# Layer-3 local attention: dividing after the context instead of before, with the row sums taken by TensorE

## The chip, the cores and the metric

One core of one Trainium2 chip runs the whole kernel in one launch. The metric is device time in microseconds (us), from start to end of that launch; the median of three runs stands for a kernel. One more execution was recorded by the profiler, and every duration below is from it.

## What is computed

The network has four layers, each an attention-like part times the silu of a feed-forward-like part, added to the input. The change lies in the second part of layer 3 (`_L3_ffn_ref`), which is itself a two-layer local transformer (DEPTH 2, 8 heads of 64, windows of 64 positions). Per layer of it:

```
q = l2norm(q) * qs;  k = l2norm(k) * ksc;  q, k = rotary_xpos(q, k)
sim  = einsum('bhwid,bhwjd->bhwij', 8 * bq, bk)      # keys: window before and own window, 128
sim  = where(mask, -max, sim)
attn = softmax(sim, axis=-1)
out  = einsum('bhwij,bhwjd->bhwid', attn, bv)
x = x + out @ wo ... then a layer norm and a gelu feed-forward part
```

## The kernel before, in words

The network runs in a loop of 8 chunks of 512 tokens (2 sequences of 256) for layers 0 and 1, then layer 2, then again 8 chunks for layer 3. In each of those last 8 chunks `layer3_attention` runs first and `layer3_ffn` (line 1589 on) second. `layer3_ffn` goes twice through `for l in range(DEPTH)`, so what is told here happens 16 times in a run. All data is f32, with features or queries on the 128 partitions.

Each engine has its own written-out list of instructions, in program order; nothing is scheduled by a tool. Engines wait for each other by semaphores (`wait_ge`), and `link` makes an engine wait for its own last instruction. So what stands behind a waiting instruction on its engine waits too.

One pass through `l` has four pieces. First the projections: TensorE (L1612, L1618), squares on ScalarE (L1722), rotary products on VectorE (L1789), their sums on GpSimd (L1859, L1860), the norms (L1603, L1708 to L1713) and the normalised keys and queries on VectorE (L1777). Second the **attention stage**, on which the change works. Third the output projection (L1680) and the residual sum (L1817 to L1820). Fourth layer norm and feed-forward part.

The attention stage handles A = 8 units; a unit is two heads (hp) of one sequence (sq) with 4 windows of 64 queries, laid out as 128 rows (2 heads x 64 queries) by 512 columns (4 windows x 128 keys). A unit m passes through these steps:

- **scores** (PE, L1631 and, for the mask, L1635), made for two units at once, into PSUM banks 0, 1, 5, 7. The scores of a pair need the exponentials two pairs back to be done (`win_exped`), because they take their banks.
- **row maximum** (DVE, L1803) and its product with -8 (DVE, L1805).
- **exponentials** (ACT, L1743, four instructions) into buffer PP of four slots.
- **row sum** (DVE, L1812), **reciprocal** of 4 sums per row (DVE, L1813), and **product** of the exponentials with it (POOL, L1864).
- **transposes** (PE, L1660, four of 128x128), copied from PSUM to PT by ACT (L1736).
- **context** (PE, L1674, eight products, values times PT) into bank 4 or 6. Both sequences of a head pair share a bank: 512 columns.
- **copy** of the finished head pair to OF (DVE, L1800), once per two units.

Each engine takes these steps of different units in a fixed interleaving, `for m in range(A + 4)` on PE and ACT and `range(A + 5)` on DVE: in turn m, PE makes the scores of m and m+1 (m even), the transposes of m-3 and the context of m-4; ACT copies the transposes of m-4 and then exponentiates m; DVE copies the context of m-5 (where it ends a head pair), takes the maximum of m and then the sum and reciprocal of m-1. At m = 0 and 1 DVE also makes the last two normalised tiles (L1777). After the eight products L1864 of the first layer GpSimd issues eight gathers for the next chunk (`gather_mixed`, L1430).

Of the kernel before, what the change touches and what calls it, by code (L numbers as in the profile page):

```python
# [8 lines left out]
ALU = mybir.AluOpType  # L9
ACT = mybir.ActivationFunctionType  # L10
AX = mybir.AxisListType

D = 128
SEQ = 256
NB = 2
T = NB * SEQ
# [13 lines left out]
DEPTH, LH, LD, WIN = 2, 8, 64, 64  # L30
LI = LH * LD
# [1406 lines left out]
def layer3_attention(nc, c, w, r, it, x_mid, s_mid, PB):  # L1438
    with ExitStack() as ctx:
# [20 lines left out]
        with nc.Block() as block:  # L1460
# [107 lines left out]
L3F_SEMS = (LN_SEMS + GATE_SEMS + LINKS + "pad_set shift_done raw_ready squared multiplied norm_ready norm_taken rnorm_ready "  # L1568
            "first_turned second_turned both_ready v_ready v_copied win_ready win_max win_exped win_recip prob_ready probT_ready "
            "probT_copied ctx_ready ctx_copied o_ready x_added hn_ready gate_in_ready gelu_done val_ready hid_ready "  # L1570
            "out_ready layer_done x_done xT_ready x_copied x_stored places_copied ")
NW = SEQ // WIN
SCORES = 4
SCORE_BANKS = (0, 1, 5, 7)
NT = LI // 128
# [3 lines left out]
def layer3_ffn(nc, c, ws, r, soft, it, out, ys_mid, PB):  # L1579
    with ExitStack() as ctx:  # L1580
        s = record(**semaphores(nc, ctx, L3F_SEMS)._asdict(), gathered=soft.soft0)
        b = buffers(nc, ctx, "l3f", HS=[NB, SEQ], HN=[T], SQ=[2, 2, T], CS=[2, 4, T], NR=[2, T], RN=[2, T],
                    QK=[2 * NT, T], VL=[NB, 3, LI], MX=[NW], MN=[SCORES, NW], SM=[NW], RS=[SCORES, NW], PP=[SCORES, T], PT=[2, T], OF=[NT, T],
                    G=[3, T], HH=[3, T])
        F = c.XN
        U, A, P = 2 * NT, NT * NB, NT
        VALUES = ((0, 1), (2, 3), (4,), (5,))

        with nc.Block() as block:
            @block.tensor  # L1590
            def _(pe):
                for l in range(DEPTH):
                    w, u0, a0 = ws[l], l * U, l * A
# [43 lines left out]

                    for m in range(A + 4):
                        if m < A and m % 2 == 0:
                            if m == 0:  # L1640
                                pe.wait_ge(s.multiplied, u0 + U - 2)
                            if m == 2:
                                pe.wait_ge(s.norm_taken, l * P + P)
                                pe.wait_ge(s.v_copied, NB * 3 * (l + 1))
                            if m % 4 == 0:
                                pe.wait_ge(s.both_ready, l * P + 2 * (m // 4) + 2)
                            if m >= SCORES:
                                pe.wait_ge(s.win_exped, a0 + m - SCORES + 2)
                            scores(m)
                            if m == 0:  # L1650
                                norm(P - 1)
                        v = m - 3
                        if 0 <= v < A:
                            if v == 0:
                                pe.wait_ge(s.multiplied, u0 + U)
                            pe.wait_ge(s.prob_ready, a0 + v + 1)
                            if v >= 2:
                                pe.wait_ge(s.probT_copied, a0 + v - 1)
                            for win in range(NW):
                                last = nc.tensor.transpose(PB[:, 2 + v % 2, win * 128:(win + 1) * 128],  # L1660
                                                           b.PP[:, v % SCORES, win * 128:(win + 1) * 128], c.ident)
                            last.then_inc(s.probT_ready, 1)
                        v = m - 4
                        if 0 <= v < A:
                            hp, sq = 2 * (v // 4) + v % 2, v // 2 % 2
                            if sq == 0 and hp >= 2:
                                pe.wait_ge(s.ctx_copied, l * NT + hp - 1)
                            pe.wait_ge(s.probT_copied, a0 + v + 1)
                            k = 4 + 2 * (hp % 2)
                            for win in range(NW):  # L1670
                                for h in range(2):
                                    f0 = (2 * hp + h) * LD
                                    o0 = sq * SEQ + win * WIN
                                    last = nc.tensor.matmul(PB[LD * h:LD * h + LD, k, o0:o0 + WIN], b.VL[:, sq, max(win - 1, 0), f0:f0 + LD],  # L1674
                                                            b.PT[:, v % 2, win * 128 + h * WIN:win * 128 + h * WIN + WIN],
                                                            start=True, stop=True, tile_position=(0, LD * h))
                            last.then_inc(s.ctx_ready, 1)
                    for t in range(NT):
                        pe.wait_ge(s.ctx_copied, l * NT + max(t + 1, NT - 1))
                        last = nc.tensor.matmul(PB[:, 4, :], w.o[:, t * 128:(t + 1) * 128], b.OF[:, t, :], start=t == 0, stop=t == NT - 1)  # L1680
# [20 lines left out]
            def _(act):  # L1701
                link = Link(act, s.act_link)
                act.preload_act_table_set(EXP_LN)
                for l in range(DEPTH):
# [24 lines left out]

                    for m in range(A + 4):  # L1730
                        v = m - 4
                        if v >= 0:
# [24 lines left out]
            def _(dve):  # L1757
# [10 lines left out]
                for l in range(DEPTH):  # L1768
# [25 lines left out]

                    for m in range(A + 5):
                        v = m - 5
                        if 0 <= v and v // 2 % 2:
                            hp = 2 * (v // 4) + v % 2
                            dve.wait_ge(s.ctx_ready, a0 + v + 1)
                            nc.vector.tensor_copy(b.OF[:, hp, :], PB[:, 4 + 2 * (hp % 2), :]).then_inc(s.ctx_copied, 1)  # L1800
                        if m < A:
# [5 lines left out]
                            if m < 2:  # L1807
                                normalised(P - 2 + m)
                        v = m - 1
                        if 0 <= v < A:  # L1810
                            dve.wait_ge(s.win_exped, a0 + v + 1)
                            link(nc.vector.tensor_reduce(b.SM[:], b.PP[:, v % SCORES, :].rearrange("p (w k) -> p w k", k=128), AX.X, ALU.add))  # L1812
                            nc.vector.reciprocal(b.RS[:, v % SCORES, :], b.SM[:]).then_inc(s.win_recip, 1)  # L1813
                            dve.wait_ge(s.win_recip, a0 + v + 1)
                    dve.wait_ge(s.o_ready, l + 1)
# [34 lines left out]
            def _(pool):  # L1850
# [3 lines left out]
                for l in range(DEPTH):  # L1854
                    u0 = l * U
                    for i in range(P):
                        if i < P:
                            pool.wait_ge(s.multiplied, u0 + 2 * i + 2)
                            nc.gpsimd.tensor_tensor(b.CS[:, i % 2, 0, :], b.CS[:, i % 2, 0, :], b.CS[:, i % 2, 3, :], ALU.subtract).then_inc(s.first_turned, 1)  # L1859
                            nc.gpsimd.tensor_tensor(b.CS[:, i % 2, 2, :], b.CS[:, i % 2, 2, :], b.CS[:, i % 2, 1, :], ALU.add).then_inc(s.second_turned, 1)  # L1860
                    for m in range(A):
                        pool.wait_ge(s.win_recip, l * A + m + 1)
                        pp = b.PP[:, m % SCORES, :].rearrange("p (w k) -> p w k", k=128)
                        nc.gpsimd.tensor_tensor(pp, pp, b.RS[:, m % SCORES, :].unsqueeze(2).broadcast_to([128, NW, 128]),  # L1864
                                                ALU.mult).then_inc(s.prob_ready, 1)
                    if l == 0:
# [296 lines left out]
```

## Time and profile before

| | |
|---|---|
| median of 3 runs | 4228.34 us (4226.57 to 4237.04) |
| the profiled execution: its time / its span | 4234.82 us / 4233.2 us |
| PE busy | 3121.1 us, 74% |
| DVE busy | 2419.7 us, 57% |
| ACT busy | 1756.8 us, 42% |
| POOL busy | 1192.0 us, 28% |

The span is the time from the first to the last recorded instruction, and the busy shares are means over stages with different limits. A busy share below 100% on all engines means that at each moment one of them waits for another; which one, in the stage in question, is read from the order of time.

### The profile page before, as it was taken

What the parts mean: (1) busy time and instruction counts of PE and PEld (TensorE: products, weight loads), DVE (VectorE), ACT (ScalarE), POOL (GpSimd) and SP (SyncE); (2) the same over time, 40 slices, a digit from 0 to 9 for tenths busy, and PEclk for the clock granted to TensorE, in tenths of its full rate; (3) what the DMA queues carried; (4) which work ended last, traced back from release to release, by engine and by line L of the source; (5) the groups of instructions that cost most, each with busy time, mean ns of one, the idle gap of its engine ahead of it and who ended that gap; (6) DMA issues with size and microseconds to landing.
All of it is one profiled execution on the core that took longest, in us unless ns stands there. A gap on an engine that the chain in (4) does not pass through costs nothing. (4 is left out here: it accounts for less than half of the span.)

```text
span 4233.2 us, 54691 instructions
## 1 busy us (share of the span) xinstructions
PE 3121.1 (74%) x20450; PEld 1694.0 (40%) x20450; DVE 2419.7 (57%) x3405; ACT 1756.8 (42%) x3556; POOL 1192.0 (28%) x878
## 2 busy tenths in 40 slices
PE   6788888887343778888767678676786867768687
PEld 3444444444131333444334344343443434434344
DVE  2344444444263778778855665556665565656655
ACT  2333333333132555556434434344343444535344
POOL 0000000000232454445543243332433324233242
PEclk7888888888655889999878879688796887969779
DMA  2000000000121222333300000000000000000001
GB/s 95 8 7 5 3 7 7 7 7 5 65 92 50 69 74 75 92 88 88 84 18 6 9 1 6 8 6 9 1 6 8 6 9 1 6 8 6 8 1 8
DMA packets 82171, 112.05 MB, mean 26 GB/s; under 512 B 9920, under 2 KB 47296, under 8 KB 81344
## 3 DMA queue, kind: packets, MB, share of 16 engines
q1 hardware_dynamic: 76608, 98.31, 7.7%
q0 software_dynamic: 5376, 11.02, 1.1%
q8 instruction: 145, 2.38, 0.2%
q14 instruction: 42, 0.34, 0.0%
HBM read 82.55 MB, written 26.74 MB: 26 GB/s over the span
## 5 line engine op out<-in xcount | busy, mean ns | idle before, releaser
L370 ACT ACTIVATE l_PT<-PB 128x512 f32<-128x512 f32 x512 | 277.9, 595 | 542.0 <-PE PB L281 542.0
L281 PE MATMUL PB<-l_QM,l_KP 32*128 32x256 f32 x2048 | 375.0, 496 | 131.6 <-DVE l_QM L419 76.0
L1412 POOL TENSOR_TENSOR l_ST<-l_ST,l_CT 128x1024 f32<-128x1024 f32 x128 | 316.4, 2472 | 354.3 <-DVE l_ST L1351 354.3
L408 DVE TENSOR_REDUCE keep_MXP<-PB 128x4 f32<-128x1024 f32 x256 | 301.3, 1219 | 109.1 <-PE PB L254 109.1
L1351 DVE TENSOR_TENSOR_SCAN l_ST<-l_DA,l_DB 128x1024 f32<-128x1024 f32 x128 | 355.6, 2778 | 4.4
L281 PEld LDWEIGHTS PB<-l_QM,l_KP 32*128 32x128 f32 x2048 | 242.7, 244 | 258.7 <-ACT l_PT L370 98.6
L704 POOL MEMSET l_KV<- 128x4 f32 x8 | 0.8, 104 | 941.3 <-POOLq L109 941.3
L1563 POOL TENSOR_TENSOR l_PT<-l_PT,l_PEN 128x512 f32<-128x512 f32 x168 | 213.1, 1290 | 186.0 <-ACT l_PT L370 186.0
L1345 DVE TENSOR_TENSOR l_DB<-PB,l_BT 128x1024 f32<-128x1024 f32 x128 | 155.3, 1213 | 137.5 <-PE PB L1111 137.5
L1274 ACT ACTIVATE l_DA<-PB,keep_aneg 128x510 f32<-128x510 f32 x256 | 161.1, 683 | 160.2 <-DVE l_ST L1351 83.4
L295 PE MATMUL PB<-l_PT,keep_VT 128*32 128x256 f32 x2048 | 187.6, 529 | 35.5 <-POOL l_PT L1563 25.6
L1743 ACT ACTIVATE l3f_PP<-PB,l3f_MN 128x128 f32<-128x128 f32 x512 | 145.6, 367 | 160.0 <-DVE l3f_MN L1805 160.0
L254 PE MATMUL PB<-l_KP,l_QP 32*128 32x256 f32 x2048 | 199.8, 518 | 15.6 <-issue 15.6
L1789 DVE SCALAR_TENSOR_TENSOR l3f_CS<-PB,w3fs,consts 128x512 f32<-128x512 f32 x256 | 175.2, 745 | 54.7 <-ACT l3f_SQ L1722 51.4
L1111 PE MATMUL PB<-l_DL,consts 32*128 32x512 f32 x512 | 166.0, 686 | 52.8 <-ACT l_DA L1274 37.7
L419 DVE TENSOR_TENSOR l_QM<-l_QP,PB 128x256 f32<-128x256 f32 x128 | 53.9, 421 | 258.5 <-PE PB L263 255.0
L1864 POOL TENSOR_TENSOR l3f_PP<-l3f_PP,l3f_RS 128x512 f32<-128x512 f32 x128 | 133.1, 1040 | 219.9 <-DVE l3f_RS L1813 219.9
L1859 POOL TENSOR_TENSOR l3f_CS<-l3f_CS 128x512 f32<-128x512 f32 x64 | 81.0, 1266 | 340.2 <-DVE l3f_CS L1789 340.2
L1612 PE MATMUL PB<-l3f_HS,w3fs 128*128 128x512 f32 x256 | 136.3, 659 | 35.9 <-DVE l3f_HS L1762 23.0
L1631 PE MATMUL PB<-l3f_QK 32*64 32x128 f32 x4096 | 138.8, 287 | 32.0 <-ACT l3f_NR L1708 26.0
L1111 PE MATMUL PB<-l_DU,consts 32*128 32x512 f32 x512 | 159.3, 682 | 0.0
L1449 POOL TENSOR_SCALAR l_T<-l_AJ,l_GI 128x256 f32<-128x256 f32 x16 | 18.3, 1146 | 478.8 <-DVE l_AJ L1539 478.8
(419 smaller groups left out, 6771.5 us busy)
## 6 DMA issues: line engine op xcount, KB each, us to landing
l_WB<-in_w2f_dram SPq DMA_DIRECT2D x80, 320.0 KB, 3.0
l_WB<-in_w2f_dram SPq DMA_DIRECT2D x80, 258.0 KB, 2.7
l_XR<-xs_mid SPq DMA_DIRECT2D x80, 64.0 KB, 1.8
ys_mid<-l_YO SPq DMA_DIRECT2D x80, 64.0 KB, 2.8
s_mid<-keep_S SPq DMA_DIRECT2D x17, 256.0 KB, 2.0
w3fs<-in_w3f_dram SPq DMA_DIRECT2D x1, 3127.0 KB, 18.1
keep_XI<-in_x_dram SPq DMA_DIRECT2D x9, 256.0 KB, 3.1
x_mid<-keep_X SPq DMA_DIRECT2D x9, 256.0 KB, 3.1
```

Source lines behind the costliest of these rows:

```text
L254: last = nc.tensor.matmul(PB[:, r, qt * SEQ:(qt + 1) * SEQ], b.QP[rows, a, q0:q0 + 128], b.KP[rows, a, i, sq * SEQ:(sq + 1) * SEQ], start= ...
L281: last = nc.tensor.matmul(PB[:, 4 + u % STBANKS, kt * SEQ:(kt + 1) * SEQ], b.KP[rows, a, i, k0:k0 + 128], b.QM[rows, n % 2, :], start=True ...
L295: last = nc.tensor.matmul(PB[32 * r:32 * r + 32, 7, 0:SEQ], VT[:, 2 * sq + kt, 8 * a + 2 * r + i, :], b.PT[:, (NR * (2 * j + i) + r) % PSL ...
L370: nc.scalar.activation(b.PT[:, u % PSLOTS].rearrange("p k q -> p (k q)"), PB[:, 4 + u % STBANKS, :], ACT.Exp).then_inc(s.exp_done, 1)
L408: nc.vector.tensor_reduce(dst[:, 2 * pair:2 * pair + 2, :, 16 + n % 2], PB[:, 2 * pair:2 * pair + 2, :].rearrange("p r (t k) -> p r t k", ...
L1111: return nc.tensor.matmul(PB[:, bank + e, :], c.rowsel[q:q + 32, i * 128:(i + 1) * 128], src[q:q + 32, k % 2, h, :], start=True, stop=True)
L1274: last = nc.scalar.activation(b.DA[:, g % 2, e, :].rearrange("p (s t) -> p s t", t=SEQ)[:, :, 1:SEQ], PB[:, e, :].rearrange("p (s t) -> p ...
L1345: nc.vector.tensor_tensor(b.DB[:, g % 2], PB[:, PAIR0:PAIR0 + 2, :], b.BT[:, k % 2, :].unsqueeze(1).broadcast_to([128, 2, T]), ALU.mult).t ...
L1351: nc.vector.tensor_tensor_scan(b.ST[:, g % RING].rearrange("p k t -> p (k t)"), b.DA[:, g % 2].rearrange("p k t -> p (k t)"), b.DB[:, g % ...
L1412: nc.gpsimd.tensor_tensor(b.ST[:, g % RING], b.ST[:, g % RING], b.CT[:, k % 2, :].unsqueeze(1).broadcast_to([128, 2, T]), ALU.mult).then_i ...
L1563: nc.gpsimd.tensor_tensor(pt, pt, b.PEN[:, 2 * sq:2 * sq + 2, :], ALU.mult).then_inc(s.weighed_pool, 1)
L1789: last = nc.vector.scalar_tensor_tensor(out=seq(b.CS[:, i % 2, 2 * half + j, :]), in0=seq(PB[:, 2 * (i % 2) + half, :]), scalar=scale, in1 ...
```

## The change

The exponentials are no longer divided before they are transposed. PE transposes them as ScalarE wrote them and multiplies them with the values; two more products per unit, with a matrix of ones as the stationary side (L1677 of the changed kernel), give the row sums, each sum standing on the 64 partitions of its head and on the column of its query, beside the context. DVE then takes the reciprocal of these 128x256 sums and multiplies the 128x256 context by it. GpSimd has nothing left to do in the stage. Each unit now has a bank half of its own (columns 0 to 255 for the context, 256 to 511 for the sums), and banks 4 and 6 alternate from unit to unit. The transposes, context and division of a unit each stand one turn earlier in the loops than the transposes, context and copy did.

```
@@ PE
-                    for m in range(A + 4):
+                    for m in range(A + 3):
...
-                        v = m - 3
+                        v = m - 2
...
-                            pe.wait_ge(s.prob_ready, a0 + v + 1)
+                            pe.wait_ge(s.win_exped, a0 + v + 1)
...
-                        v = m - 4
+                        v = m - 3
...
-                            if sq == 0 and hp >= 2:
-                                pe.wait_ge(s.ctx_copied, l * NT + hp - 1)
+                            if v >= 2:
+                                pe.wait_ge(s.ctx_divided, a0 + v - 1)
                             pe.wait_ge(s.probT_copied, a0 + v + 1)
-                            k = 4 + 2 * (hp % 2)
+                            k = 4 + 2 * (v % 2)
...
+                            for h in range(2):
+                                last = nc.tensor.matmul(PB[LD * h:LD * h + LD, k, SEQ:2 * SEQ], c.ones[:, 0:LD],
+                                                        b.PT[:, v % 2, :].rearrange("p (w h q) -> p h w q", h=2, q=WIN)[:, h],
+                                                        start=True, stop=True, tile_position=(0, LD * h))
                             last.then_inc(s.ctx_ready, 1)
                     for t in range(NT):
-                        pe.wait_ge(s.ctx_copied, l * NT + max(t + 1, NT - 1))
+                        pe.wait_ge(s.ctx_divided, a0 + A - (t < NT - 1))
@@ ACT
-                    for m in range(A + 4):
-                        v = m - 4
+                    for m in range(A + 3):
+                        v = m - 3
@@ DVE
-                    for m in range(A + 5):
-                        v = m - 5
-                        if 0 <= v and v // 2 % 2:
-                            hp = 2 * (v // 4) + v % 2
+                    for m in range(A + 4):
+                        v = m - 4
+                        if 0 <= v:
+                            hp, sq = 2 * (v // 4) + v % 2, v // 2 % 2
                             dve.wait_ge(s.ctx_ready, a0 + v + 1)
-                            nc.vector.tensor_copy(b.OF[:, hp, :], PB[:, 4 + 2 * (hp % 2), :]).then_inc(s.ctx_copied, 1)
+                            link(nc.vector.reciprocal(b.RD[:], PB[:, 4 + 2 * (v % 2), SEQ:2 * SEQ]))
+                            nc.vector.tensor_tensor(b.OF[:, hp, sq * SEQ:(sq + 1) * SEQ], PB[:, 4 + 2 * (v % 2), 0:SEQ], b.RD[:],
+                                                    ALU.mult).then_inc(s.ctx_divided, 1)
+                            dve.wait_ge(s.ctx_divided, a0 + v + 1)
...
-                            dve.wait_ge(s.win_exped, a0 + v + 1)
-                            link(nc.vector.tensor_reduce(b.SM[:], b.PP[:, v % SCORES, :].rearrange("p (w k) -> p w k", k=128), AX.X, ALU.add))
-                            nc.vector.reciprocal(b.RS[:, v % SCORES, :], b.SM[:]).then_inc(s.win_recip, 1)
-                            dve.wait_ge(s.win_recip, a0 + v + 1)
@@ POOL
-                    for m in range(A):
-                        pool.wait_ge(s.win_recip, l * A + m + 1)
-                        pp = b.PP[:, m % SCORES, :].rearrange("p (w k) -> p w k", k=128)
-                        nc.gpsimd.tensor_tensor(pp, pp, b.RS[:, m % SCORES, :].unsqueeze(2).broadcast_to([128, NW, 128]),
-                                                ALU.mult).then_inc(s.prob_ready, 1)
```

How this moves instructions on TensorE (PE), from the second pair of scores of a stage on; before:

```order
L1631 MATMUL PB<-l3f_QK 64x128 x32
L1635 MATMUL PB<-windowb,identb 128x512 x2
L1660 MATMUL PB<-consts,l3f_PP 128x128 x4
L1631 MATMUL PB<-l3f_QK 64x128 x32
L1635 MATMUL PB<-windowb,identb 128x512 x2
L1660 MATMUL PB<-consts,l3f_PP 128x128 x4
L1674 MATMUL PB<-l3f_PT,l3f_VL 64x64 x8
L1660 MATMUL PB<-consts,l3f_PP 128x128 x4
L1674 MATMUL PB<-l3f_PT,l3f_VL 64x64 x8
```

and now, from the same pair of scores on:

```order
L1631 MATMUL PB<-l3f_QK 64x128 x32
L1635 MATMUL PB<-windowb,identb 128x512 x2
L1660 MATMUL PB<-consts,l3f_PP 128x128 x8
L1673 MATMUL PB<-l3f_PT,l3f_VL 64x64 x8
L1677 MATMUL PB<-l3f_PT,consts 64x256 x2
L1631 MATMUL PB<-l3f_QK 64x128 x32
L1635 MATMUL PB<-windowb,identb 128x512 x2
L1660 MATMUL PB<-consts,l3f_PP 128x128 x4
L1673 MATMUL PB<-l3f_PT,l3f_VL 64x64 x8
L1677 MATMUL PB<-l3f_PT,consts 64x256 x2
```

Ahead of the third pair of scores there stood the transposes of one unit; now there stand the transposes of two units and the whole context of the first, with its two products by ones.

On VectorE (DVE), from the maximum of the fourth unit on; before:

```order
L1803 TENSOR_REDUCE l3f_MX<-PB 128x4
L1805 TENSOR_SCALAR l3f_MN<-l3f_MX 128x4
L1812 TENSOR_REDUCE l3f_SM<-l3f_PP 128x4
L1813 RECIPROCAL l3f_RS<-l3f_SM 128x4
L1803 TENSOR_REDUCE l3f_MX<-PB 128x4
L1805 TENSOR_SCALAR l3f_MN<-l3f_MX 128x4
```

and now:

```order
L1809 TENSOR_REDUCE l3f_MX<-PB 128x4
L1811 TENSOR_SCALAR l3f_MN<-l3f_MX 128x4
L1803 RECIPROCAL l3f_RD<-PB 128x256
L1804 TENSOR_TENSOR l3f_OF<-PB,l3f_RD 128x256
L1809 TENSOR_REDUCE l3f_MX<-PB 128x4
L1811 TENSOR_SCALAR l3f_MN<-l3f_MX 128x4
```

The sum and the small reciprocal of the unit before are gone from between two maxima, and the large reciprocal and the product of the unit four back have come there; the copies L1800 are gone too.

## Rows read from the trace of the kernel before

**Rows 1.** The page's head: span, busy time of each engine.
```profile
span 4233.2 us, 54691 instructions
...
PE 3121.1 (74%) x20450; PEld 1694.0 (40%) x20450; DVE 2419.7 (57%) x3405; ACT 1756.8 (42%) x3556; POOL 1192.0 (28%) x878
```
**Rows 2.** Chain of work, last attention stage: start us, us, what.
```profile
4189.59 0.69 PE PB L1674 x16
4190.27 1.91 PE PB L1631 x64
```
**Rows 3.** Timeline, last attention stage: start us, us, engine line op [idle before].
```profile
4173.03 1.98 PE L1631 MATMUL PB<-l3f_QK 32*64 32x128 f32 x64 [0.37 <-DVE l3f_QK L1777]
...
4181.68 0.68 DVE L1812 TENSOR_REDUCE l3f_SM<-l3f_PP 128x4 f32<-128x512 f32 x1
...
4187.90 0.69 DVE L1812 TENSOR_REDUCE l3f_SM<-l3f_PP 128x4 f32<-128x512 f32 x1
4187.90 1.14 ACT L1743 ACTIVATE l3f_PP<-PB,l3f_MN 128x128 f32<-128x128 f32 x4 [0.45 <-DVE l3f_MN L1805]
...
4189.98 0.69 DVE L1812 TENSOR_REDUCE l3f_SM<-l3f_PP 128x4 f32<-128x512 f32 x1
...
4205.47 0.68 DVE L1817 TENSOR_TENSOR l3f_HS<-keep_XN,PB 64x512 f32<-64x512 f32 x1 [3.10 <-PE PB L1680]
```
**Rows 4.** The same timeline: TensorE's steps and who follows them.
```profile
4192.11 0.61 PE L1635 MATMUL PB<-windowb,identb 128*128 128x512 bf16 x2
...
4192.55 0.60 PE L1660 MATMUL PB<-consts,l3f_PP 128*128 128x128 f32 x4
...
4193.08 0.69 PE L1674 MATMUL PB<-l3f_PT,l3f_VL 128*64 128x64 f32 x16
...
4193.70 0.66 PE L1660 MATMUL PB<-consts,l3f_PP 128*128 128x128 f32 x4
...
4200.19 1.44 PE L1674 MATMUL PB<-l3f_PT,l3f_VL 128*64 128x64 f32 x32
...
4200.99 1.38 DVE L1800 COPY l3f_OF<-PB 128x512 f32<-128x512 f32 x2 [2.56 <-PE PB L1674]
...
4201.73 3.70 PE L1680 MATMUL PB<-l3f_OF,w3fs 128*128 128x512 f32 x8
```
**Rows 5.** Groups by line and form: busy us, mean ns, idle before.
```profile
L1864 POOL TENSOR_TENSOR l3f_PP<-l3f_PP,l3f_RS 128x512 f32<-128x512 f32 x128 | 133.1, 1040 | 219.9 <-DVE l3f_RS L1813 219.9
...
L1803 DVE TENSOR_REDUCE l3f_MX<-PB 128x4 f32<-128x512 f32 x128 | 88.0, 687 | 44.6 <-PE PB L1635 42.4
...
L1736 ACT ACTIVATE l3f_PT<-PB 128x512 f32<-128x512 f32 x128 | 76.0, 611 | 26.8 <-PE PB L1660 26.8
...
L1800 DVE COPY l3f_OF<-PB 128x512 f32<-128x512 f32 x64 | 44.2, 692 | 64.5 <-PE PB L1674 49.8 <-remote 13.6
...
L1813 DVE RECIPROCAL l3f_RS<-l3f_SM 128x4 f32<-128x4 f32 x128 | 22.8, 178 | 4.4
...
L157 DVE SCALAR_TENSOR_TENSOR l3f_HN<-PB,keep_lnt 128x256 f32<-128x256 f32 x32 | 13.6, 424 | 1.1
...
L871 DVE TENSOR_REDUCE l2r_M<-l2r_LO 128x4 f32<-128x64 f32 x8 | 1.8, 220 | 0.3
...
L1961 DVE TENSOR_TENSOR w3fs<-w3fs,PB 128x1 f32<-128x1 f32 x4 | 0.6, 146 | 0.0
```
**Rows 6.** Line L1805: duration ns least/median/longest over all stages.
```profile
L1805 DVE TENSOR_SCALAR l3f_MN<-l3f_MX x128: 170/364/739, 2266.0 to 4195.8; 128x4 f32<-128x4 f32 x128
```
**Rows 7.** Timeline of a first-layer stage: slow scores, gathers beside a copy.
```profile
3065.92 3.44 PE L1631 MATMUL PB<-l3f_QK 32*64 32x128 f32 x64
...
3086.54 0.94 POOL L1430 DMA_INDIRECT keep_YG<-ys_mid,places  x1 [0.30 <-issue]
...
3086.91 0.69 DVE L1800 COPY l3f_OF<-PB 128x512 f32<-128x512 f32 x1 [1.43 <-remote]
```
**Rows 8.** Windows view of those scores: us, busy by engine, granted clock (PEclk), DMA.
```profile
3065.90:3069.30 3.40, 3.40 (x66) 3.05 (x65) 2.18 (x6) 2.14 (x8) 2.00 (x2) 0.55 0.02 5
```

More of the change, by code:

```diff
@@ L1568 @@
 L3F_SEMS = (LN_SEMS + GATE_SEMS + LINKS + "pad_set shift_done raw_ready squared multiplied norm_ready norm_taken rnorm_ready "
-            "first_turned second_turned both_ready v_ready v_copied win_ready win_max win_exped win_recip prob_ready probT_ready "
-            "probT_copied ctx_ready ctx_copied o_ready x_added hn_ready gate_in_ready gelu_done val_ready hid_ready "
+            "first_turned second_turned both_ready v_ready v_copied win_ready win_max win_exped probT_ready "
+            "probT_copied ctx_ready ctx_divided o_ready x_added hn_ready gate_in_ready gelu_done val_ready hid_ready "
             "out_ready layer_done x_done xT_ready x_copied x_stored places_copied ")
@@ L1582, in layer3_ffn @@
         b = buffers(nc, ctx, "l3f", HS=[NB, SEQ], HN=[T], SQ=[2, 2, T], CS=[2, 4, T], NR=[2, T], RN=[2, T],
-                    QK=[2 * NT, T], VL=[NB, 3, LI], MX=[NW], MN=[SCORES, NW], SM=[NW], RS=[SCORES, NW], PP=[SCORES, T], PT=[2, T], OF=[NT, T],
+                    QK=[2 * NT, T], VL=[NB, 3, LI], MX=[NW], MN=[SCORES, NW], RD=[SEQ], PP=[SCORES, T], PT=[2, T], OF=[NT, T],
                     G=[3, T], HH=[3, T])
@@ L1672, in _ @@
                                     f0 = (2 * hp + h) * LD
-                                    o0 = sq * SEQ + win * WIN
-                                    last = nc.tensor.matmul(PB[LD * h:LD * h + LD, k, o0:o0 + WIN], b.VL[:, sq, max(win - 1, 0), f0:f0 + LD],
+                                    nc.tensor.matmul(PB[LD * h:LD * h + LD, k, win * WIN:win * WIN + WIN], b.VL[:, sq, max(win - 1, 0), f0:f0 + LD],
                                                             b.PT[:, v % 2, win * 128 + h * WIN:win * 128 + h * WIN + WIN],
                                                             start=True, stop=True, tile_position=(0, LD * h))
+                            for h in range(2):
+                                last = nc.tensor.matmul(PB[LD * h:LD * h + LD, k, SEQ:2 * SEQ], c.ones[:, 0:LD],
+                                                        b.PT[:, v % 2, :].rearrange("p (w h q) -> p h w q", h=2, q=WIN)[:, h],
+                                                        start=True, stop=True, tile_position=(0, LD * h))
                             last.then_inc(s.ctx_ready, 1)
                     for t in range(NT):
-                        pe.wait_ge(s.ctx_copied, l * NT + max(t + 1, NT - 1))
+                        pe.wait_ge(s.ctx_divided, a0 + A - (t < NT - 1))
                         last = nc.tensor.matmul(PB[:, 4, :], w.o[:, t * 128:(t + 1) * 128], b.OF[:, t, :], start=t == 0, stop=t == NT - 1)
@@ L1808, in _ @@
                                 normalised(P - 2 + m)
-                        v = m - 1
-                        if 0 <= v < A:
-                            dve.wait_ge(s.win_exped, a0 + v + 1)
-                            link(nc.vector.tensor_reduce(b.SM[:], b.PP[:, v % SCORES, :].rearrange("p (w k) -> p w k", k=128), AX.X, ALU.add))
-                            nc.vector.reciprocal(b.RS[:, v % SCORES, :], b.SM[:]).then_inc(s.win_recip, 1)
-                            dve.wait_ge(s.win_recip, a0 + v + 1)
                     dve.wait_ge(s.o_ready, l + 1)
```

## The prediction

> **What bounds the kernel now.** I read the page's head first [rows 1]: no engine is near full, PE with 74% of 4233.2 us is the busiest, and that mean says nothing about the stage that changes. So I took the last attention stage alone: its chain of waits [rows 2] and its order of time [rows 3, 4]. From the first scores at 4173.03 to the residual sum at 4205.47 it takes 32.44 us, and there are 16 of them, some 520 us, 12% of the run. In its middle VectorE sets the pace: two row sums stand at 4187.90 and 4189.98, 2.08 us apart, and between them lie a sum, a small reciprocal, a maximum and the product with -8. The chain leaves DVE only where the order of PE and ACT forces a detour: transposes copied by ACT, context on PE, and then the next scores, which stand behind that context in PE's list [rows 2]. So there are two limits close together: DVE's own work per unit, and a loop PE, DVE, ACT, PE, ACT, PE that a unit runs through. GpSimd's product takes 1.04 us per unit and GpSimd idles 219.9 us before it [rows 5]: it is no bound, only a step on the way.
>
> **What the change takes away.** Per unit: the row sum 0.69 [rows 3], the small reciprocal 0.178, half of a 0.692 copy [rows 5], and on GpSimd 1.04 us. With the gaps that is 2.08 + 0.35 = 2.43 us of DVE per unit down to maximum and product alone. The product with -8 is at best 170 ns, but at the median 364 and at most 739 [rows 6]; it lasts longer where GpSimd works, so I give it 0.17 from here on. Maximum and product then take 0.92 us with their semaphores.
>
> **What it adds on DVE.** A product of 128x256, for which the nearest row is 0.424 us [rows 5], 0.46 with its gap, and a reciprocal of 128x256, of which the trace has no example: only one of 4 elements, 178 ns [rows 5]. This is the price that decides. Reductions give the fixed part of an instruction and its cost per element: 220 ns for 64 elements, 687 for 512 [rows 5], so 1.04 ns per element and 153 fixed. By that fixed part the reciprocal has 25 ns for four elements, 6.2 each, and 256 cost 0.153 + 1.6 = 1.75 us. If it ran at the pace of all others, one element per 1.04 ns, it would be 0.42, the lower end. If the fixed part is that of the shortest instruction with operands, 146 ns for one element [rows 5], so 145, then 33 ns are left for four, 8.2 each, and 256 cost 2.25 us, the upper end. In between lies the product with -8 of the same four elements, 170 ns [rows 6]: by it only 8 ns are extra, 3 ns per element in all, 0.95 us. I take 1.75, because reductions read one tensor and wait for nothing else, like a reciprocal, and because 0.42 leaves 20 of the 178 ns unexplained.
>
> The Trainium skill has a rule here that speaks against the change: its page "VectorE: DVE Perf Modes", section "First, the fixed hardware budget", says that Reciprocal is an iterative divide with a repeat count of 8. Read as eight cycles of the page's 0.96 GHz per element, that would be an estimated 2.28 us, the rival of the upper end below; no row here shows more than four elements.
>
> **What it adds on PE.** Two products of 256 columns per unit, each issued as two passes. A pass of 512 columns takes 0.43 us (eight of them in 3.70 [rows 4], the last one's tail included), so four passes of 256 take 0.85 one after another. But the context's 16 passes of 64 columns, 0.85 by the same rate, take 0.62 from 4193.08 to 4193.70 [rows 4]: the two halves of the array work side by side. So 0.43 to 0.85; I take 0.5.
>
> **The sum: one stage walked through.** Times are from the stage's first scores. PE's steps: scores of a pair 1.91 [rows 2] and 0.44 for the mask, 2.35; transposes 0.53; context 0.62 [rows 4] and 0.5, 1.11 together; from a context's start to DVE 0.80 [rows 4] and 0.5, so 1.3.
> - DVE finishes its last normalised tile at 8.65 (4181.68 [rows 3]); nothing before that changes. Third maximum and product: 9.6. ACT's exponentials 1.14 [rows 3] to 10.75. Behind them stands the copy of the first transposes, 0.61 [rows 5], to 11.4. Context on PE, and DVE's first reciprocal starts at 12.7.
> - Reciprocal and product take 1.75 + 0.06 + 0.46 = 2.27: 14.97, and the next maximum 15.9. Meanwhile PE does the third pair of scores, which now stand behind the context: 12.5 + 2.35, transposes 0.53, then the second context at 15.4; DVE can go on at 16.7, ends at 18.96.
> - Three turns of 0.92 + 2.27 = 3.19: 28.5. Here DVE is the bound.
> - The sixth context waits for the last exponentials and ACT's copy: DVE goes on at 29.4. Two times 2.27: 33.9. The output projection may start, its last part hides the eighth division (2.27 against 2.56). From there 3.74 us to the residual sum [rows 4]: 37.7.
>
> Against 32.44 that is +5.3; the same walk with the old order comes out at 32.7, so I take 5.1 per stage, 16 x 5.1 = +82 us.
>
> Two edits with no sum of their own. The gathers of the next chunk stood behind the eight GpSimd products in the first of the two layers; with those gone they start when the rotary sums end, about 5 us into the stage, and run for 8 x 1.25 = 10 us. Before, one copy waited 1.43 us beside them [rows 7]; now the copies are gone, and instead three products with -8 lie beside the gathers. I let one and the other cancel; if only the gain remained, it would be 8 x 1.4 = 11 us. And in that layer one pair of scores took 3.44 us, where the same step in other stages takes 1.98 [rows 7, 3]: the granted clock was 0.55 there [rows 8], close to the lower of its two levels (1.2 of 2.4 GHz), after PE had idled. Idle time now falls in two shorter pieces, because transposes come in between; at most another 8 x 1.5 = 12 us less, in which I don't trust. GpSimd's product is nowhere missed: it was off the path except for its delay, which the walk already leaves out.
>
> So 4234.82 + 82 = 4317 for the profiled execution; the median of the runs lies 6.5 below that execution: **4310 us**.
>
> **The rivals.**
> - *Eight cycles per element.* Reciprocal 2.25: each turn 3.69. The same walk gives 12.7, 15.5, 16.7, 19.5, 30.5, 30.9, 36.4, and now the eighth division ends at 39.2, later than the projection's first three parts; the residual sum at 40.4. Less the same 0.2 that is +7.8 per stage, +125: 4353. For it: the upper end of the rows. Against it: the fixed part would have to be the least seen.
> - *The reciprocal runs like any other instruction.* With 0.42 DVE is free, yet the stage isn't shorter. The third pair of scores still can't start before 12.5, because a context with its ones and the transposes of two units stand before it; the fourth starts at about 18.6, where it started at 17.2 before (4190.2 [rows 2]); the rest takes as long as before. +1.3 per stage, +21: 4249. At 0.95 it is +2.6, +42: 4270. For it: the 8 ns against the product with -8.
> - *DVE's freed time comes through* (the faster side). If DVE's work per unit is all that matters, then at 0.42 a unit costs 0.92 + 0.94 = 1.86 instead of 2.43, so 0.57 x 8 x 16 = 73 us less: 4155. It decides from a reciprocal below 0.99 us on, and needs PE's scores not to be held by the context before them. The chain through PE between 4189.59 and 4192 [rows 2] speaks against it: that detour already exists and gets longer.
> - *The change does nothing here* because all this lies beside other work: excluded, the chain of waits runs through the stage from end to end.
>
> **How the numbers follow.** Reciprocal near 1.75: 0.50. Near 2.25: 0.25. Between 0.42 and 0.95 with PE as the bound: 0.18. DVE's time comes through: 0.07. The likeliest gives 4310, with 4285 to 4335 for the ones at 0.43 to 0.85 us and the gathers either way. The range leaves out the faster side and the very lowest of the third case, and ends above 4353 by the same spread: 4250 to 4365. A measurement of this kernel can tell some 0.3% (13 us) from no change. Faster by more: 0.07. Within 0.3%: 0.05, the lowest part of the third case with the gathers' gain. Slower: 0.88.
>
> **What would show it.** In the profile after: the group of the reciprocal at 1.7 to 1.8 us mean (2.25 or 0.42 for the rivals); DVE's maxima 3.2 us apart in the middle of a stage; DVE busy up, by 128 x (1.75 + 0.42 - 0.69 - 0.18 - 0.35 - 0.16) = 101 us, to 2520; a stage of 37.5 us; PE busy up, POOL down by 133. ScalarE waiting for PE or DVE in every turn. Wrong would be the walk if the reciprocal is 1.75 and the stages are still below 35 us or above 40, and the choice of price if the reciprocal is elsewhere.

## The result and the profile after

The changed kernel takes **4317.93 us**, median of 4 runs (4311.35 to 4324.31), the kernel before 4227.45 beside it (4 runs, 4203.07 to 4237.04): ratio 1.0223, 95% interval 1.0177 to 1.0269. So it is slower, by about 94 us; 4310 was forecast. Below, a ratio leaves out executions that ran over 1.5% above the fastest of their kernel at a lower clock (one of e7's, one of e8's, two of e11's), while a median is that of all. The profiled execution took 4311.35 us. The head of its page, against [rows 1]:

```profile
span 4309.1 us, 55483 instructions
...
PE 3145.9 (73%) x20858; PEld 1707.7 (40%) x20962; DVE 2536.5 (59%) x3341; ACT 1756.8 (41%) x3556; POOL 1068.7 (25%) x750
```

DVE has 116.8 us more, POOL 123.3 less. The groups by line and form (as in [rows 5]: busy us and mean ns of one, then the engine's idle us just before them and what ended it):

```profile
L1803 DVE RECIPROCAL l3f_RD<-PB 128x256 f32<-128x256 f32 x128 | 224.9, 1757 | 90.8 <-PE PB L1677 53.5 <-remote 34.6
...
L1809 DVE TENSOR_REDUCE l3f_MX<-PB 128x4 f32<-128x512 f32 x128 | 88.0, 688 | 26.8 <-remote 22.6 <-PE PB L1635 1.7
...
L1677 PE MATMUL PB<-l3f_PT,consts 128*64 128x256 f32 x512 | 83.1, 398 | 0.0
...
L1804 DVE TENSOR_TENSOR l3f_OF<-PB,l3f_RD 128x256 f32<-128x256 f32 x128 | 54.3, 424 | 4.4
```

The price that had to be chosen is in the first row: 1757 ns per reciprocal. The column of idle time has something new beside it: 34.6 us before the reciprocals and 22.6 before the maxima end in "remote", an event that no instruction in the trace explains ("issue" stands where the engine waited for nothing that the trace shows), where the maxima of before waited for PE [rows 5].

The timeline of the last stage, the one that the prediction walked through (answers to [rows 3, 4]):

```profile
4244.07 1.98 PE L1631 MATMUL PB<-l3f_QK 32*64 32x128 f32 x64 [0.37 <-DVE l3f_QK L1780]
...
4255.34 0.69 PE L1673 MATMUL PB<-l3f_PT,l3f_VL 128*64 128x64 f32 x16 [2.02 <-ACT l3f_PT L1739]
...
4256.39 1.98 PE L1631 MATMUL PB<-l3f_QK 32*64 32x128 f32 x64
...
4256.57 1.76 DVE L1803 RECIPROCAL l3f_RD<-PB 128x256 f32<-128x256 f32 x1 [2.02 <-PE PB L1677]
...
4260.50 1.76 DVE L1803 RECIPROCAL l3f_RD<-PB 128x256 f32<-128x256 f32 x1 [0.78 <-PE PB L1677]
...
4262.75 0.69 DVE L1809 TENSOR_REDUCE l3f_MX<-PB 128x4 f32<-128x512 f32 x1
...
4265.93 0.69 DVE L1809 TENSOR_REDUCE l3f_MX<-PB 128x4 f32<-128x512 f32 x1
...
4269.11 0.69 DVE L1809 TENSOR_REDUCE l3f_MX<-PB 128x4 f32<-128x512 f32 x1
...
4277.56 3.70 PE L1683 MATMUL PB<-l3f_OF,w3fs 128*128 128x512 f32 x8 [1.13 <-DVE l3f_OF L1804]
...
4281.37 0.68 DVE L1817 TENSOR_TENSOR l3f_HS<-keep_XN,PB 64x512 f32<-64x512 f32 x1 [1.61 <-PE PB L1683]
```

The stage runs from 4244.07 to 4281.37, 37.30 us against 32.44. The first reciprocal starts 12.50 us in, the second 16.43 us in, and the maxima then stand 3.18 us apart. Between two of them the chain of waits now lies on DVE alone:

```profile
4262.30 0.43 DVE l3f_OF L1804
4262.75 0.70 DVE l3f_MX L1809
4263.48 0.18 DVE l3f_MN L1811
4263.68 1.77 DVE l3f_RD L1803
```

The windows view of whole stages, the last first-layer one and the last second-layer one; before, then after. Its columns: the stretch, its length, the busy us of PE, of PE's weight loads, of DVE, ACT and POOL (instructions in brackets), the granted clock of PE as a share of 2.4 GHz, the busy share of the DMA engines, GB/s:

```profile
4102.36:4137.57 35.21, 26.60 (x436) 18.81 (x436) 23.47 (x43) 16.93 (x46) 17.39 (x17) 0.95 0.13 9
4173.03:4205.47 32.44, 25.05 (x436) 17.51 (x436) 23.63 (x42) 16.94 (x46) 11.78 (x11) 1.00 0.01 2
```

```profile
4164.28:4208.60 44.32, 32.26 (x464) 21.44 (x468) 31.08 (x38) 16.91 (x46) 11.95 (x11) 0.88 0.23 13
4244.07:4281.37 37.30, 27.53 (x464) 18.60 (x468) 30.79 (x38) 16.76 (x46) 3.48 (x3) 1.00 0.01 2
```

Both layers have the same busy time on DVE (31.08 and 30.79 us), yet the first layer's stage is 7.0 us longer. It is the one with the gathers, and its mean clock is 0.88. Its timeline:

```profile
4169.68 1.86 POOL L1430 DMA_INDIRECT keep_YG<-ys_mid,places  x1 [0.15 <-issue]
...
4174.67 0.69 DVE L1809 TENSOR_REDUCE l3f_MX<-PB 128x4 f32<-128x512 f32 x1 [1.57 <-remote]
...
4177.28 1.12 PE L1673 MATMUL PB<-l3f_PT,l3f_VL 128*64 128x64 f32 x16 [3.76 <-issue]
...
4179.19 2.40 PE L1631 MATMUL PB<-l3f_QK 32*64 32x128 f32 x17
...
4181.84 2.86 PE L1631 MATMUL PB<-l3f_QK 32*64 32x128 f32 x47 [0.25 <-issue]
4182.04 1.76 DVE L1803 RECIPROCAL l3f_RD<-PB 128x256 f32<-128x256 f32 x1 [5.50 <-remote]
...
4187.73 1.76 DVE L1803 RECIPROCAL l3f_RD<-PB 128x256 f32<-128x256 f32 x1 [1.50 <-PE PB L1677]
...
4208.60 0.68 DVE L1817 TENSOR_TENSOR l3f_HS<-keep_XN,PB 64x512 f32<-64x512 f32 x1 [1.61 <-PE PB L1683]
```

and the same stretch in windows of 4 us:

```profile
4174.00:4178.00 4.00, 0.72 (x14) 0.72 (x16) 1.76 (x4) 2.40 (x9) 2.88 (x4) 0.79 0.78 43
4178.00:4182.00 4.00, 3.62 (x33) 1.77 (x33) 0.00 (x0) 0.86 (x3) 1.89 (x2) 0.50 0.88 40
4182.00:4186.00 4.00, 3.67 (x51) 3.20 (x53) 2.84 (x3) 0.00 (x0) 0.00 (x0) 0.50 0.63 30
```

While the gathers keep the DMA engines 0.78 to 0.88 busy, PE does 0.72 us of work in four, then runs at the lower clock level (0.50 of 2.4 GHz) for eight us.

The second reciprocal waits for PE. It starts 23.45 us into this stage and 16.43 us into the other, so all 7.0 us arise before it. On PE they are these: the first context starts 1.7 us later; from there to the third pair of scores it takes 0.9 us longer; the scores themselves take 5.5 us instead of 1.98; and 0.9 us more go by from there to the reciprocal. The scores are slow by more than their clock: in the rows above 17 of their 64 products take 2.40 us, the other 47 only 2.86, although nothing in the trace holds either. The waits of 3.76 and 5.50 us are to be set against 2.02 and 2.02 us at the same places of the stage without gathers.

Summed over the 16 stages (first scores to residual sum) the two profiles give 546.6 and 654.4 us, +107.8. But ahead of the first stage, in code that nobody touched, the profiled execution of after took 2236.2 us against 2262.7. Over all profiles of this study that part varies between 2234.7 and 2269.5, with no order in it. So the +76 us between the two spans understate the change; stage lengths repeat to tenths of a microsecond and are the better gauge of a stage.

### The profile page after: what moved, and what is told of

It reads as the page before. It is cut to its first block and busy times, and to the rows that moved or that the text cites. A ratio compares the mean times of both kernels' runs of the same rounds, so it can differ in the third digit from the quotient of the medians.

```text
span 4309.1 us, 55483 instructions
## 1 busy us (share of the span) xinstructions
PE 3145.9 (73%) x20858; PEld 1707.7 (40%) x20962; DVE 2536.5 (59%) x3341; ACT 1756.8 (41%) x3556; POOL 1068.7 (25%) x750
## 5 line engine op out<-in xcount | busy, mean ns | idle before, releaser
L281 PE MATMUL PB<-l_QM,l_KP 32*128 32x256 f32 x2048 | 362.0, 482 | 131.8 <-DVE l_QM L419 76.1
L1803 DVE RECIPROCAL l3f_RD<-PB 128x256 f32<-128x256 f32 x128 | 224.9, 1757 | 90.8 <-PE PB L1677 53.5
L1631 PE MATMUL PB<-l3f_QK 32*64 32x128 f32 x4096 | 150.5, 289 | 40.7 <-ACT l3f_NR L1711 26.1
L1673 PE MATMUL PB<-l3f_PT,l3f_VL 128*64 128x64 f32 x2048 | 91.6, 234 | 109.3 <-ACT l3f_PT L1739 89.6
```

The lines of the kernel that those rows point to most:

```text
L281: last = nc.tensor.matmul(PB[:, 4 + u % STBANKS, kt * SEQ:(kt + 1) * SEQ], b.KP[rows, a, i, k0:k0 + 128], b.QM[rows, n % 2, :], start=True ...
L1803: link(nc.vector.reciprocal(b.RD[:], PB[:, 4 + 2 * (v % 2), SEQ:2 * SEQ]))
```

## The experiments

All stage lengths of the study in one place, as read from the timelines; outliers in brackets. "Layer" is the first (with gathers) or the second of the two that share the loop.

| kernel | first layer, us | second layer, us | sum of 16 | ratio to before |
|---|---|---|---|---|
| before | 35.2 (one 39.2) | 32.44 (one 33.9) | 546.6 | 1 |
| after | 44.2 (two 43.6) | 37.30 (one 40.6) | 654.4 | 1.0223 |
| e1 late gather | 40.6 (one 38.9) | 37.31 (one 38.9) | 623.3 | 1.0176 |
| e2 copy | 39.5 to 40.1 | 33.85 (three 35.4) | 595.3 | 1.0107 |
| e3 copy, no ones | 37.9 | 33.27 | 569.7 | one run |
| e4 before, late gather | 33.9 (one 34.9) | 33.7 to 33.9 | 542.3 | 1.0005 |
| e5 busy, late gather | 37.30 | 37.30 | 596.8 | one run |
| e6 copy, old turns | 41.0 to 41.3 | 31.97 | 585.3 | one run |
| e7 before, new turns | 36.9 to 38.3 | 31.12 to 33.9 | 560.6 | 1.0019 |
| e8 sums by ScalarE | 34.15 (32.8 to 36.5) | 29.99 (one 31.8) | 513.9 | 0.9954 |
| e9 busy, early gather | 43.7 to 44.6 | 37.29 | 651.4 | one run |
| e10 before, busy | 33.9 (three 38.2 to 39.8) | 32.44 or 33.9 | 552.5 | one run |
| e11 e8 and busy | 32.7 to 34.9 | 29.98 or 31.43 | 518.9 | 0.9951 |
| e12 e8, late gather | 29.97 or 31.60 | 29.97 or 31.60 | 492.6 | 0.9904 |

### e1: the gathers at the end of the stage

```
                         pool.wait_ge(s.places_copied, 1)
+                        pool.wait_ge(s.ctx_divided, A - 1)
```

> The changed kernel, but the eight gathers for the next chunk wait for the seventh divided context, so they run about where they ran before the change. In the changed kernel the first-layer stages take 44.2 us and the second-layer ones 37.3, and the sum of the prediction had no term for that difference. Theory (gathers beside the early attention delay VectorE, then TensorE idles and falls to its lower clock): first-layer stages come down from 44.2 to between 37.3 and 39.5, second-layer ones stay at 37.3, the run gets 8 x 5 to 7 = 40 to 55 us shorter than the changed kernel, about 1.0% over the kernel before. Rival (the first-layer stages are longer because of TensorE's clock alone, whatever the gathers do): 44.2 stays within 1 us and the run stays where it is.

Measured: 4292.59 us (4 runs), ratio 1.0176, interval 1.0096 to 1.0257. That is less than expected: some 20 us below the changed kernel by the two ratios, whose intervals overlap, where 40 to 55 were forecast; the sum of the stages is 31 us shorter. First-layer stages fell from 44.2 to 40.6, not to 39.5 or less. The other 3.3 us show in its last first-layer stage: the third pair of scores, then its window, then the output projection:

```profile
4190.16 3.07 PE L1631 MATMUL PB<-l3f_QK 32*64 32x128 f32 x64
...
4212.43 5.40 PE L1683 MATMUL PB<-l3f_OF,w3fs 128*128 128x512 f32 x8 [1.13 <-DVE l3f_OF L1804]
```

```profile
4188.00:4192.00 4.00, 3.41 (x56) 2.65 (x60) 1.65 (x1) 2.06 (x7) 0.00 (x0) 0.63 0.02 4
```

The scores take 3.07 instead of 1.98 and the projection 5.40 instead of 3.70, at a clock of 0.63 with the DMA engines idle (0.02). Two causes, then: the gathers, and a clock that falls there even with the gathers gone.

### e2 and e3: the reciprocal's price, and the ones

```
-    link(nc.vector.reciprocal(b.RD[:], PB[:, 4 + 2 * (v % 2), SEQ:2 * SEQ]))
+    link(nc.vector.tensor_copy(b.RD[:], PB[:, 4 + 2 * (v % 2), SEQ:2 * SEQ]))
```

e2 multiplies by the sum where the kernel divides by it; e3 leaves the products with ones out too, and copies columns 0 to SEQ.

> The changed kernel with the reciprocal of the sums left out: a copy of the same 128x256 sums stands in its place, so the output is not divided rightly. Theory (1.76 us of reciprocal per unit makes VectorE the bound, the rest is the loop through TensorE): the copy takes 0.42 us, second-layer stages come down from 37.3 to 33.8, still 1.3 over the 32.44 of before. Rival (VectorE's freed time comes through once the reciprocal is cheap): second-layer stages go to about 28 us, below before by 4.6.

> As the copy kernel, and the two products by ones are left out too; the copy reads the context instead of the sums. Theory: with the products by ones (0.5 us each unit) off the loop through TensorE, second-layer stages come to about 31.3 us, 2.5 below the copy kernel. Rival (the products by ones lie beside other work): no change against the copy kernel, within 0.3 us per stage.

The copy's line in e2, duration least/median/longest:

```profile
L1803 DVE COPY l3f_RD<-PB x128: 424/425/426, 2264.7 to 4226.6; 128x256 f32<-128x256 f32 x128
```

e2: 4260.06 us (4 runs), ratio 1.0107, interval 1.0034 to 1.0179; second-layer stages 33.85. So 1.33 us saved per unit, 10.7 per stage, bring 3.45 of the 37.30, and the stage is still 1.4 longer than before. That is what the prediction's walk gave for a reciprocal at 0.42: PE's order binds. e3 missed: second-layer stages of 33.27 instead of 31.3. The ones were to be worth 2.5 us per stage; only 0.6 came. Two rows of the last stage show most of the rest:

```profile
4209.15 0.90 PE L1673 MATMUL PB<-l3f_PT,l3f_VL 128*64 128x64 f32 x16 [2.03 <-ACT l3f_PT L1735]
...
4209.98 3.36 PE L1631 MATMUL PB<-l3f_QK 32*64 32x128 f32 x64
```

The scores took 3.36 instead of 1.98: 1.4 of the missing 2 us are the clock's. In e3 they take 3.2 to 3.5 us in all eight second-layer stages, in e2 1.98 in five and 2.8 to 2.9 in three. But the idling alone doesn't decide: e2's last stage has the same 2.03 us in the same place and keeps its speed. In e3 the context right behind the idling is already slow (0.90 instead of 0.69), before the missing products by ones would have run. That less work on PE is the reason is thus likely, not shown. The run gained nothing by e3's shorter stages: it took 4260.48 us (one run), as long as e2.

### e4 and e10: the same two causes in the kernel before

```
                         pool.wait_ge(s.places_copied, 1)
+                        pool.wait_ge(s.o_ready, 1)
```

> The kernel before, with its eight gathers put off until the output projection is done. Theory (beside the gathers two copies of the context wait, 1.3 us per first-layer stage): first-layer stages 35.2 to 33.9, the run 8 x 1.3 = 10 us shorter, if nothing in the layer norm behind them waits instead. Rival (the wait moves to the layer norm and feed-forward part): stages shorter, the run the same within 5 us.

4218.68 us (10 runs), ratio 1.0005, interval 0.9967 to 1.0043: no gain in the run. First-layer stages became 1.3 us shorter as expected, but second-layer ones, which have no gathers, 1.3 us longer; this row of the last one has their third pair of scores:

```profile
4163.68 2.97 PE L1631 MATMUL PB<-l3f_QK 32*64 32x128 f32 x64
```

The slow scores [rows 7, 8] moved from one stage of the kernel before into most of them. What decides this was not found.

e10 keeps PE busy at that point, with 8 products of a mask that nobody reads:

```
+    if m == 3:
+        for _ in range(8):
+            nc.tensor.matmul(PB[:, 6, :], c.identb, c.windowb, start=True, stop=True)
```

> The kernel before with eight such products in the idle time ahead of the first transposes (2.4 us). First-layer stages take 35.2 us there, with one pair of scores at 3.44 instead of 1.98. Theory (clock): that pair comes to 1.98 and first-layer stages to 33.7; second-layer stages stay at 32.44. Rival (the products push the transposes back as much as they save): no change within 0.3.

4225.89 us, one run. Those scores took 1.98 and five of eight first-layer stages were 33.9, but in the other three, of 38.2 to 39.8 us, the output projection spanned 6.1 to 8.0 us instead of 3.70, because DVE's last copies, which it needs, stood beside the gathers (one idled 5.70 us before it, to "remote"); and five second-layer ones took 33.9: no gain in the sum (552.5 against 546.6).

### e5 and e9: PE kept busy in the changed kernel

The same 8 products ahead of the first context: e5 with the late gathers of e1, e9 with the gathers where the change has them.

> The changed kernel with its gathers late, as in the run of that name, and eight products of 128x512 in bf16 that nobody reads, put into TensorE's idle time ahead of the first context (2.0 us there). With late gathers first-layer stages take 40.6 us and second-layer ones 37.3; the scores after the first context take 3.07 instead of 1.98 us in the first and the output projection 5.40 instead of 3.70. Theory (those 3.3 us are TensorE's lower clock after its idle time): first-layer stages come to between 37.3 and 39.0. Rival (the clock there follows something further back): they stay at 40.6 within 0.3.

> The changed kernel with the same eight unread products in TensorE's idle time, but with the gathers where the change put them, 5.4 us into the stage. With them and without the products a first-layer stage takes 44.2 us; with late gathers and the products 37.3. Theory (of the 6.9 us, 3.3 are the clock and 3.6 the gathers' delay of VectorE and what follows it): 40.5 to 41.5 us. Rival (the gathers' only effect is the idle time that lowers the clock, which the products fill): 37.3 to 38.5.

e5, one run, 4285.97 us: all 16 stages 37.30. The timeline and windows of its last first-layer stage:

```profile
4155.65 1.89 PE L1665 MATMUL PB<-windowb,identb 128*128 128x512 bf16 x8
...
4158.88 1.98 PE L1631 MATMUL PB<-l3f_QK 32*64 32x128 f32 x64
```

```profile
4146.60:4183.90 37.30, 29.22 (x472) 19.32 (x476) 30.79 (x39) 16.71 (x46) 5.91 (x6) 1.00 0.03 4
```

Products that nobody reads take 1.89 us on PE and cost nothing, since they fill the idling; the granted clock stays at 1.00, and first and second layer are alike. Of the first layer's 6.9 us, late gathers thus take 3.6 off and busy products the other 3.3. e9 missed: 44.1 us on average, nothing gained, where 40.5 to 41.5 had been expected. So the two causes don't add up. With the gathers in the middle, DVE is held up for longer than 8 products last, and PE's scores, which wait for no engine, come in pieces; 6 of the 64 products begin in the first 2.6 us:

```profile
4178.06 0.51 PE L1631 MATMUL PB<-l3f_QK 32*64 32x128 f32 x3
...
4180.67 3.57 PE L1631 MATMUL PB<-l3f_QK 32*64 32x128 f32 x58 [0.34 <-issue]
...
4180.95 1.76 DVE L1806 RECIPROCAL l3f_RD<-PB 128x256 f32<-128x256 f32 x1 [5.62 <-remote]
```

```profile
4177.00:4181.00 4.00, 2.75 (x34) 1.82 (x38) 0.05 (x1) 1.59 (x5) 1.78 (x2) 0.66 0.96 42
```

The DMA share is 0.96 there and DVE waits 5.62 us. What such a wait waits for stays open: the trace calls its end only "remote" or "issue", and no run separates GpSimd's issuing of the gathers (0.95 us each) from their transfers. The one packet of the instruction queue in that stretch of the changed kernel falls after 4183 us, when DVE had gone on at 4182.04, so nothing in the trace ties that wait to it.

### e6 and e7: the turns alone

e6 is e2 with transposes, context and division one turn later again (`v = m - 2` back to `m - 3` and so on), where the kernel before has them. e7 is the kernel before with ACT's copy one turn earlier (`v = m - 4` to `m - 3`) and DVE's copy one later.

> The copy kernel (no reciprocal, output not divided rightly), with transposes, context and division each one turn later, where transposes, context and copy stood before the change. Theory (the context that now stands ahead of the third pair of scores holds them): second-layer stages 33.84 less 1.7, some 32.1 us. Rival (only the work per engine counts, turns don't matter): 33.84 within 0.3.

> The kernel before with two turns moved: ACT copies the transposes of a unit one turn earlier, ahead of the exponentials of the next, and DVE copies a finished context one turn later, behind the next maximum. Nothing is added or left out. Theory (the stage is bound in part by the order of waits): second-layer stages 32.44 less 1.8, 30.6 us, the run some 30 us shorter. Rival (DVE's work per unit is the bound, 2.08 us): 32.4 within 0.3.

e6, one run, 4266.88 us: second layer 31.97, hit, so the earlier turns cost 1.9 us of e2's 33.85, as long as the reciprocal is cheap. First layer 41.2, longer than e2's: not explained. e7, 4238.49 us (10 runs), ratio 1.0019, interval 0.9987 to 1.0051, missed: the best stages are 31.12, 1.3 shorter than before, but the second layer's spread up to 33.9 and the first layer's are 36.9 to 38.3, longer than before. The third pair of scores takes 3.0 to 3.6 us instead of 1.98 in all first-layer stages and in six of the eight others: there the shorter order was paid back in clock. The first layer's stages lose by the gathers too: in the last of them a copy of the context stands beside them, DVE idles 3.64 us before it ("remote"), and the projection spans 5.5 us instead of 3.70.

### e8, e11 and e12: the sums out of the exponentials

If DVE's row sum is what to get rid of, ScalarE can give it as a second output of the exponential:

```
-    scale=8.0, bias=b.MN[:, m % SCORES, win:win + 1])
+    scale=8.0, bias=b.MN[:, m % SCORES, win:win + 1],
+    accum_out=b.SM[:, m % SCORES, win:win + 1])
...
-    link(nc.vector.tensor_reduce(b.SM[:], ...))
-    nc.vector.reciprocal(b.RS[:, v % SCORES, :], b.SM[:]).then_inc(s.win_recip, 1)
+    nc.vector.reciprocal(b.RS[:, v % SCORES, :], b.SM[:, v % SCORES, :]).then_inc(s.win_recip, 1)
```

All three have e7's turns; e11 adds e10's products, e12 the late gathers of e4.

> The same two turns moved, and the row sums are no longer taken by DVE but come out of ScalarE's exponentials as their accumulated output; DVE keeps the reciprocal of four sums, GpSimd the product. Theory (the exact division was cheap where it was, the expensive DVE step was the sum of 0.69 us): second-layer stages 28.7 us, 3.7 less than before, the run some 50 to 60 us shorter than before (ratio 0.987), if accumulating costs ScalarE less than 0.1 us per instruction. Rival (accumulating costs ScalarE more than the 0.69 us per unit that DVE saves): stages at 30.6 or above.

> The kernel with the row sums from ScalarE and the two moved turns, with the same products ahead of the first transposes. Its first-layer stages take 32.8 to 36.5 us, its second-layer ones 30.0. Theory: first-layer stages come to about 31.5 (30.0 and the wait beside the gathers), the run 10 to 25 us shorter than without the products, ratio to before 0.990 to 0.995. Rival: the idle time there is already short enough (1.7 us) and nothing changes.

> The kernel with the row sums from ScalarE and the two moved turns (first-layer stages 32.8 to 36.5 us, second-layer ones 30.0), with the gathers put off until the output projection is done. Theory (the first-layer stages are longer because the gathers run beside their end): they come to 30.0 to 31.5, the run 10 to 25 us shorter than without this, ratio to before about 0.990. Rival (as with the kernel before, what the stage gains is lost behind it or in the next stage's clock): ratio 0.995 as without it.

e8: 4201.64 us (12 runs), ratio 0.9954, interval 0.9925 to 0.9983; a gain, but a smaller one than the 0.987 expected, and second-layer stages of 29.99 instead of 28.7. The sum has a price on ScalarE, an instruction of its own:

```profile
L1743 ACT ACTIVATION_READ_ACCUMULATOR l3f_PP<-PB,l3f_MN 128x1 f32 x512 | 113.4, 222 | 0.0
```

e11: 4209.61 (12 runs), 0.9951, interval 0.9925 to 0.9976: the busy products bring nothing that shows. e12: 4171.54 (6 runs), **0.9904**, interval 0.9867 to 0.994, as expected and the lowest ratio of the study: about 1% below the kernel before. Its interval overlaps those of e8 and e11, so that it beats them is shown by the sum of its stages alone, 21 us below e8's and 26 below e11's. Its stages are 29.97 or 31.60 in both layers; the last:

```profile
4121.60:4153.20 31.60, 25.69 (x432) 18.78 (x436) 18.37 (x35) 19.48 (x78) 11.73 (x11) 0.95 0.01 2
```

DVE is busy for 18.37 us of it (30.79 in the changed kernel's last stage, 23.63 before).

## Why the prediction was right, and where it was not

- **The reciprocal's price: right.** 1.75 was taken, 1757 ns measured. The way there held: (1757 - 153) / 256 is 6.3 ns per element against 6.2 from one row of four elements. Trusting the fixed part of the reductions was the right choice among the three. That it came out to within 10 ns is luck in part: 1 ns more or less in the fixed part moves this forecast by 63 ns, and the small reciprocal reads SBUF, the large one PSUM. The rule of the Trainium skill's "VectorE: DVE Perf Modes", section "First, the fixed hardware budget", read as eight cycles per element, gave the estimate of 2.28 us. By the measurement that reading doesn't hold; a reciprocal is slower per element than a copy (425 ns for the same shape), but by less than that.
- **Product and ones: right.** 0.424 as forecast; the pair by ones spans 0.60 us (0.5 was taken), and at the full clock it delays the next scores by 0.5 (context start 4255.34, scores 4256.39: 1.05 against 1.11 in the walk).
- **The walk through a second-layer stage: right, step by step.** First reciprocal at 12.50 (12.7 forecast), second at 16.43 (16.7), turns of 3.18 (3.19), end at 37.30 (37.7); +4.86 against the forecast +5.1. e2 and e6 bear out what it said of a cheap reciprocal: the stage is then still 1.4 us longer than before, and the earlier turns alone cost 1.9 us.
- **Busy times: nearly.** DVE 2536.5 against 2520, POOL down by 123.3 against 133. Of the 16.5 us that DVE has over the forecast, some 10 are the product with -8, which was to fall to 0.17 us and still has a mean of 248 ns (128 x 0.078):

```profile
L1811 DVE TENSOR_SCALAR l3f_MN<-l3f_MX 128x4 f32<-128x4 f32 x128 | 31.7, 248 | 4.4
```

- **The step that failed: "I let one and the other cancel."** For the first layer's stages the gathers' earlier start was to cost nothing on balance, with a clock gain of up to 12 us in reserve. Its eight stages grew from 285.6 to 352.7 us together, by 67 instead of 41 (9.0 for a typical one), while the second layer's grew by 41 as forecast. So 26 us are missing from the sum, and all of them here. The prediction put the last stage's 32.44 us on all 16 ("some 520 us"; they took 546.6), and so never walked through a stage with gathers. Instead of three products held up for 1.4 us, everything was held up: DVE for 5.50 us instead of 2.02, PE for 3.76 instead of 2.02, and behind that PE's scores took 5.5 us instead of 1.98 at a clock of 0.50. Late gathers (e1) and PE kept busy (e5) together bring the first layer's stages to the second layer's 37.30. In e9 the busy products without late gathers bring nothing. Why engines stand still beside the gathers stays open.
- **Why 4310 still came close: luck in part.** The stages cost 107.8 us instead of 82 in the profiles. The profiled execution was 26.5 us quicker ahead of them, so its 4311.35 met the forecast 4317 by an error and a chance that cancel. The medians, 4317.93 and 4227.45, differ by 90; for that, 82 is somewhat low, 108 somewhat high, and the interval (75 to 114 us) holds both.
- **The rivals.** *Eight cycles per element* and *like any other instruction* fell with the 1757 ns. *DVE's freed time comes through* fell even with a cheap reciprocal: in e2 a unit costs DVE less than before, and the stage is longer than before. Its other condition, scores not held by the context before them, is met in e6, and there 0.5 us of the forecast 4.6 come through. *The change does nothing here* is excluded by the chain.

## What to carry to other kernels

A division moved behind a product is cheap only if the divisor stays small: here 4 reciprocals per partition and unit became 256, 178 ns became 1757, on the engine that set the pace. The price could be had from one four-element row, once the fixed part was taken from another instruction of the same engine. And a transfer whose start is set free by a removed instruction must be costed where it now lands, against every engine that waits there, and with the clock that PE falls to after idling.

## What the runs showed of the hardware

- A 128x256 f32 reciprocal on DVE out of PSUM took 1757 ns, a copy of the same shape 425.
- An exponential with a sum as second output was followed by a read of the accumulator of 222 ns, four per unit.
- While indirect gathers held the DMA engines 0.78 to 0.96 busy, DVE waited up to 5.62 us for events that the trace doesn't explain (2.02 us at the same place without gathers); in e7 and e10, whose gathers stand where they stood before the change, single waits of the same kind reach 3.64 and 5.70 us. The DMA view of the changed kernel from 4169 to 4185 us shows their queue (packets, MB, share of 16 engines' time); 0.52 MB in 16 us, so it is not the bytes that fill it:

```profile
q0 software_dynamic: 240, 0.52, 62.2%
```

- In e5, 1.89 us of useless products on PE made eight stages 3.3 us shorter than in e1; in e3, with less work on PE, the third pair of scores took 3.2 to 3.5 us in every second-layer stage, against 1.98 in most of e2's.
